# Top-64 attention: the threshold steering rounds counted from TensorE differences instead of ScalarE passes over the scores

## What is computed

```
scores = jnp.einsum('bhqd,bhkd->bhqk', Q, K) / jnp.sqrt(d)      # 32 x 16 x 256 x 256
topk_scores, topk_idx = jax.lax.top_k(scores, 64)
probs = jax.nn.softmax(topk_scores, axis=-1)
attn = einsum('bhqk,bhqkd->bhqd', probs, gather(V, topk_idx))
x = x + tanh(g_xattn) * (attn @ Wo.T + bo)        # attention of layernorm(x) and ctx
x = x + tanh(g_ffn) * ffn(layernorm(x))           # bf16 and fp8 rounding inside
```

## Time and profile before

| | |
|---|---|
| median of 3 runs | 3271.35 us (3269.1 to 3274.13) |
| the profiled execution | 3268.81 us, its span 3266.9 us |
| ScalarE busy | 2730.3 us, 84% |
| VectorE busy | 2691.6 us, 82% |
| TensorE busy | 1780.4 us, 54%, mean granted clock 0.717 |
| GpSimd busy | 966.1 us, 30% |

### The profile page before, as it was taken

One profiled execution on the slowest core, in us unless ns is written; L12 is line 12 of the kernel. 1 busy time (PEld: TensorE's weight loads), 2 busy tenths in 40 slices (PEclk: granted clock), 3 DMA queues, 4 the chain that ended last, 5 costly groups with the idle time before them and its releaser, 6 DMA issues.

```text
span 3266.9 us, 51511 instructions
## 1 busy us (share of the span) xinstructions
PE 1780.4 (54%) x7952; PEld 950.5 (29%) x7952; DVE 2691.6 (82%) x11883; ACT 2730.3 (84%) x9638; POOL 966.1 (30%) x1174
## 2 busy tenths in 40 slices
PE   3245555555465555455556556564556556454555
PEld 2122233332233233232323333332233223232222
DVE  1678888888888888888888888888888888888884
ACT  1888888998788898797889998988798788997983
POOL 5122223233222233232233223333223233232112
PEclk8567677777677777776667777767676767777777
DMA  4223332223333223331233333223333133331211
GB/s 70 38 43 60 49 47 52 52 49 63 52 52 54 45 49 63 52 55 34 48 64 56 60 48 56 48 48 64 53 49 55 33 62 61 55 54 33 40 24 46
DMA packets 451902, 166.43 MB, mean 51 GB/s; under 512 B 245616, under 2 KB 451440, under 8 KB 451520
## 3 DMA queue, kind: packets, MB, share of 16 engines
q1 hardware_dynamic: 451136, 162.38, 28.4%
q0 software_dynamic: 384, 0.33, 0.1%
HBM read 102.57 MB, written 59.24 MB: 50 GB/s over the span
## 4 chain that ended last, share of the span: by engine, by line
DVE 36%; ACT 30%; issue 17%; PE 14%; DVEq 2%; POOL 1%; ACTq 0%; DMA 0%; SPq 0%; POOLq 0%; another core or an unknown queue 0%
ACT act_junk L880 22%; DVE masked L1151 5%; DVE score_sb L1047 4%; PE ps_o L731 4%; DVE following L1157 4%; DVE masked L1146 3%; ACT unfit L891 3%; ACT pT_sb L900 2%; PE ps_a L684 2%; DVE X L1083 2%; PE ps_b L675 2%; PE ps_e L712 1%; PE ps_a L686 1%; DVE chord L1115 1%; PE ps_e L716 1%
## 5 line engine op out<-in xcount | busy, mean ns | idle before, releaser
L880 ACT ACTIVATE act_junk<-score_sb,X 128x256 int8<-128x256 f32 x3840 | 1892.1, 503 | 211.3 <-DVE X L1121 183.2
L712 PE MATMUL ps_e<-qs,ks 99*128 99x256 bf16 x1024 | 348.2, 350 | 1321.7 <-ACT pT_sb L900 1321.7
L731 PE MATMUL ps_o<-pT_sb,v_aug 128*32 128x256 f32 x2048 | 766.4, 514 | 0.5 <-ACT pT_sb L900 0.5
L880 ACT ACTIVATION_READ_ACCUMULATOR act_junk<-score_sb,X 128x1 f32 x3840 | 755.0, 197 | 0.0
L891 ACT ACTIVATE unfit<-score_sb,thr 128x256 bf16<-128x256 f32 x1024 | 463.1, 504 | 218.0 <-DVEq L1241 214.6
L1047 DVE TENSOR_SCALAR_CACHE_REDUCE score_sb<-ps_s 128x256 f32<-128x256 f32 x1024 | 418.8, 415 | 142.1 <-PE ps_s L698 140.0
L712 PEld LDWEIGHTS ps_e<-qs,ks 99*128 99x128 bf16 x1024 | 121.9, 119 | 1403.6 <-ACT unfit L891 1199.5
L1146 DVE TENSOR_SCALAR_CACHE_REDUCE masked<-score_sb,X 128x256 f32<-128x256 f32 x1024 | 426.3, 472 | 19.1 <-DVE x_res L1294 8.4
L1157 DVE MAX8 following<-masked 128x8 f32<-128x256 f32 x1024 | 357.7, 409 | 1.7 <-issue 0.7
L540 POOL CAST split<-proj 128x512 bf16<-128x512 f32 x64 | 48.0, 750 | 1042.8 <-ACT proj L866 1027.2
L716 PE MATMUL ps_e<-dropb,unfit 128*128 128x128 bf16 x2048 | 355.9, 273 | 0.0
(11 more groups left out here) (158 smaller groups left out, 3332.8 us busy)
## 6 DMA issues: line engine op xcount, KB each, us to landing
rows<-q_scr SPq DMA_DIRECT2D x192, 128.0 KB, 5.1
rows<-k_scr SPq DMA_DIRECT2D x192, 128.0 KB, 5.0
o_scr<-o_sb SPq DMA_DIRECT2D x128, 128.0 KB, 2.7
q_scr<-split SPq DMA_DIRECT2D x32, 384.0 KB, 2.7
k_scr<-split SPq DMA_DIRECT2D x32, 384.0 KB, 2.7
x_in<-in_x SPq DMA_DIRECT2D x32, 256.0 KB, 3.1
ctx_sb<-in_ctx SPq DMA_DIRECT2D x32, 256.0 KB, 2.7
v_scr<-proj SPq DMA_DIRECT2D x32, 256.0 KB, 5.8
```

Source lines behind the costliest of these rows:

```text
L712: nc.tensor.matmul(ps_e[:, n % 2, kc * TOK:(kc + 1) * TOK], ks[u][:, h, 8 * kc:8 * kc + 8, :].rearrange("d j t -> d (j t)"), qs[u][:, h, : ...
L731: ins = nc.tensor.matmul(ps_o[32 * c:32 * c + 32, half * TOK:(half + 1) * TOK], v_aug[p][:, 2 * h + kc, :], pT_sb[:, n % 2, kc * TOK:(kc + ...
L880: ins = nc.scalar.activation(act_junk[:, t, :], score_sb[:, slot, t, :], ACT.Sign, scale=-1.0, bias=X[slot % 2][:, 0, t:t + 1], accum_out= ...
```

## The change

ScalarE's counting passes over `score_sb` go. In a round TensorE transposes the thresholds (`transpose_thresholds`), ScalarE negates them into a 16x128 bf16 tile (`negate_thresholds`), and for each head TensorE forms the transposed scores in a bank of `ps_t` (`scores_by_key`) and adds the negated thresholds to all of them by a matmul whose stationary operand picks one row (`less_thresholds`). ScalarE takes one Sign of the 128x512 result into bf16 (`signs`), and TensorE sums the signs of every query over the keys with four matmuls against a column of ones (`tally`) into `ps_cnt`. VectorE reads the counts there. So that both sides see the same thresholds, they are kept as bf16 values (`stepped`, `started`).

The final counting moves from VectorE to ScalarE (`final_counts`, four tiles a round). VectorE's final tile is one product, (score <= threshold) x score, in place of the count and the 1024-wide subtraction, and two small steps are added to `final_thresholds`; a row whose 64th value is not positive counts as unsure.

PSUM is dealt out anew: three banks `ps_t` are shared by differences and exponents, counts and transposed thresholds share `ps_c`, and all projections, transposes and the second layer use the one bank `ps_a` in turn, which gives new waits between them. Exponents are two heads behind the masks in every engine. On TensorE a round is `count_round` with up to two exponents in it, then one piece of front or output work, two mixes, two scores and the transpose of the next thresholds. Projections of values run a batch earlier, and SP stores them earlier and moves `move_out` ahead of `move_values`. `settle` waits, in addition, for the final tiles of its round.

```diff
-MASK_LAG, MIX_LAG = 2, 4
+MIX_LAG = 2
+BANKS = 3
+SIGNS = 3
+JUNK = 4
...
+    return (GH * (GUIDES * (phase + 1) + r) + n) % SIGNS
...
+        ps_t = ps("ps_t", [P, BANKS, 512])
         ps_o = ps("ps_o", [P, 512])
         ps_a = ps("ps_a", [P, 512])
-        ps_b = ps("ps_b", [P, 512])
-        ps_x = ps("ps_x", [P, 512])
-        ps_xb = ps_x[:, 0:TOK].bitcast(BF16)
+        ps_c = ps("ps_c", [P, 512])
+        ps_xb = ps_a[:, 0:TOK].bitcast(BF16)
+        ps_xt = ps_c[0:GT, 0:P]
+        ps_cnt = [ps_c[:, P + GT * k:P + GT * (k + 1)] for k in range(2)]
+        ps_uns = ps_s[0:1, 0, 0:GT]
...
+                    store_values(b + 1)
                 if has(3):
                     load_front(b + 3)
                 move_maxima(b, u)
                 if has(2):
                     move_operands(b + 2)
...
+                if has(-1):
+                    move_out(b - 1)
                 if has(1):
                     move_values(b + 1, 1 - p)
-                if has(-1):
-                    move_out(b - 1)
...
+            def transpose_thresholds(i, slot, r):
+                pe.wait_ge(s_thr, GUIDES * i + r + 1)
+                pe.wait_ge(s_crd, GUIDES * i + r)
+                nc.tensor.transpose(ps_xt, X[slot][:, 0, :], ident[:]).then_inc(s_xt, 1)
+            def scores_by_key(u, g, n, bank):
+                h = head_of(g, n)
+                for kc in range(2):
+                    nc.tensor.matmul(ps_t[:, bank, kc * TOK:(kc + 1) * TOK],
+                                     ks[u][0:SPLITS, h, 8 * kc:8 * kc + 8, :].rearrange("d j t -> d (j t)"),
+                                     qs[u][0:SPLITS, h, :, :].rearrange("d j t -> d (j t)"), start=(kc == 0), stop=False,
+                                     skip_group_check=True)
+            def less_thresholds(i, r, n, bank):
+                if n == 0:
+                    pe.wait_ge(s_mx, GUIDES * i + r + 1)
+                both_chunks = minus_x[:].rearrange("t (o q) -> t o q", o=1).to_broadcast([GT, 2, P])
+                for jh in range(2):
+                    ins = nc.tensor.matmul(ps_t[:, bank, :].rearrange("p (c j q) -> p c j q", c=2, j=2)[:, :, jh, :],
+                                           identb[0:GT, 2 * n + jh:2 * n + jh + 1].to_broadcast([GT, P]), both_chunks,
+                                           start=False, stop=(jh == 1), skip_group_check=True)
+                ins.then_inc(s_R, 1)
+            def tally(i, par, r, n, buf):
+                pe.wait_ge(s_G, GUIDES * GH * i + GH * r + n + 1)
+                for jh in range(2):
+                    for kc in range(2):
+                        ins = nc.tensor.matmul(ps_cnt[par][:, 2 * n + jh:2 * n + jh + 1],
+                                               sign[:, buf, kc * TOK + jh * P:kc * TOK + jh * P + P], ones_b[:],
+                                               start=(kc == 0), stop=(kc == 1))
+                if n == GH - 1:
+                    ins.then_inc(s_cnt, 1)
...
+            def count_round(b, p, u, g, r, phase, first, second, last, middle):
+                i, slot = 2 * b + g, 2 * p + g
+                bank = [(phase + r + k) % BANKS for k in range(GH + 2)]
+                buf = [sign_buffer(phase, r, n) for n in range(GH)]
+                scores_by_key(u, g, 0, bank[0])
+                scores_by_key(u, g, 1, bank[1])
+                less_thresholds(i, r, 0, bank[0])
+                less_thresholds(i, r, 1, bank[1])
+                if last:
+                    exponent_taken(*last)
+                for n in (2, 3):
+                    scores_by_key(u, g, n, bank[n])
+                    less_thresholds(i, r, n, bank[n])
+                    tally(i, slot % 2, r, n - 2, buf[n - 2])
+                if first:
+                    exponents(*first, bank[4], False)
+                if middle:
+                    middle()
+                for n in (4, 5):
+                    tally(i, slot % 2, r, n - 2, buf[n - 2])
+                    scores_by_key(u, g, n, bank[n + 1])
+                    less_thresholds(i, r, n, bank[n + 1])
+                if first:
+                    exponent_taken(*first)
+                for n in (6, 7):
+                    scores_by_key(u, g, n, bank[n + 1])
+                    less_thresholds(i, r, n, bank[n + 1])
+                    tally(i, slot % 2, r, n - 2, buf[n - 2])
+                if second:
+                    exponents(*second, bank[9], False)
+                for n in (6, 7):
+                    tally(i, slot % 2, r, n, buf[n])
...
+                    for r in range(GUIDES):
+                        first, second = lagged(2 * r), lagged(2 * r + 1)
...
+                        middle = None
+                        if r == 0 and mixes:
+                            middle = lambda: sum_unsure(2 * mb + mg, 16 * (b + 1) + GH * g + 1 if has(1) else 16 * NB)
+                        if guided:
+                            count_round(cb, cp, cu, cg, r, phase, first, second, last, middle)
...
+                        if has(2) and (g, r) == (0, 0):
+                            transpose_tokens(b + 2)
+                        if has(2) and (g, r) == (0, 1):
+                            transpose_context(b + 2)
+                        if has(2) and (g, r) == (0, 2):
+                            project(b + 2, 0, 0)
+                        if has(-3) and (g, r) == (0, 3):
+                            ffn_transposes(b - 3, 2 * b + 5 if has(2) else 2 * NB, b + 2 if has(2) else NB, b - 2)
+                        if has(2) and (g, r) == (1, 0):
+                            project(b + 2, 1, b - 2)
+                        if has(-3) and (g, r) == (1, 1):
+                            ffn_matmul(b - 3, 2 * b + 6 if has(2) else 2 * NB)
+                        if has(-2) and (g, r) == (1, 2):
+                            out_project(b - 2, b - 2, 2 * b + 6 if has(2) else 2 * NB)
+                        if has(2) and (g, r) == (1, 3):
+                            project_values(b + 2, b - 1)
+                        if first:
+                            mix(*first)
+                        if second:
+                            mix(*second)
+                        for k in (2 * r + 2, 2 * r + 3):
+                            if k < GH and has(1):
+                                scores(b + 1, (u + 1) % OPS, g, k, 2 * b + g - 1 if k == 2 and mixes else None)
+                            if k >= GH and g == 0 and has(1):
+                                scores(b + 1, (u + 1) % OPS, 1, k - GH)
+                            if k >= GH and g == 1 and has(2):
+                                scores(b + 2, (u + 2) % OPS, 0, k - GH)
+                        if r < GUIDES - 1 and guided:
+                            transpose_thresholds(2 * cb + cg, 2 * cp + cg, r + 1)
+                        if r == GUIDES - 1 and has(1):
+                            transpose_thresholds(2 * (b + 1) + g, 2 * (1 - p) + g, 0)
...
-            def guide_counts(i, slot, r):
-                act.wait_ge(s_cnt, at(GUIDES * i + r))
-                act.wait_ge(s_thr, GUIDES * i + r + 1)
-                for t in range(ACT_TILES):
-                    ins = nc.scalar.activation(act_junk[:, t, :], score_sb[:, slot, t, :], ACT.Sign, scale=-1.0,
-                                               bias=X[slot % 2][:, 0, t:t + 1], accum_out=count[slot % 2][:, t:t + 1])
-                ins.then_inc(s_cnt, 1)
+            def negate_thresholds(i, r):
+                act.wait_ge(s_xt, GUIDES * i + r + 1)
+                nc.scalar.activation(minus_x[:], ps_xt, ACT.Copy, scale=-1.0).then_inc(s_mx, 1)
+            def signs(i, r, n, buf, bank):
+                act.wait_ge(s_R, GUIDES * GH * i + GH * r + n + 1)
+                nc.scalar.activation(sign[:, buf, :], ps_t[:, bank, :], ACT.Sign).then_inc(s_G, 1)
+            def final_counts(i, slot, t):
+                if t == 0:
+                    act.wait_ge(s_fin, FINAL * i + 1)
+                if t % JUNK == 0:
+                    act.wait_ge(s_fc, 4 * i + t // 4)
+                ins = nc.scalar.activation(act_junk[:, t % JUNK, :], score_sb[:, slot, t, :], ACT.Sign, scale=-1.0,
+                                           bias=X[slot][:, 0, t:t + 1], accum_out=final_count[:, t:t + 1])
+                if t % 4 == 3:
+                    ins.then_inc(s_fc, 1)
...
+            def round_of_signs(i, r, phase, i_final, final_slot, first, second, mixed):
+                bank = [(phase + r + k) % BANKS for k in range(GH + 2)]
+                if i is not None:
+                    negate_thresholds(i, r)
+                for n in range(GH):
+                    if i is not None:
+                        signs(i, r, n, sign_buffer(phase, r, n), bank[n if n < 4 else n + 1])
+                    if n == 3 and first:
+                        exps(*first, bank[4])
+                    if n == 3 and mixed:
+                        evacuate_mixed(*mixed)
+                    if n == 7 and second:
```

(71 more changed lines are left out.)

380 lines of the change are left out of this document (195 added, 185 removed).

## The result

| | before | after |
|---|---|---|
| median | 3270.22 us (3266.8 to 3274.13, 4 runs) | 3739.13 us (3727.18 to 3747.62, 4 runs) |
| profiled execution, span | 3266.9 us | 3733.4 us |
| TensorE busy, mean granted clock | 54%, 0.717 | 94%, 0.665 |
| ScalarE busy | 84% | 67% |
| VectorE busy | 82% | 59% |

The ratio is 1.1431, 95% interval 1.1395 to 1.1467: 14% slower. The prediction was 3145 us, range 2970 to 3340. It is wrong in sign and size.

The account below looks back on a forecast made before the run. Bound by the loop of ScalarE's counts and VectorE's threshold update, 12.05 us a round; after, 31.5 batches of 90.15 us (2840), repairs 71, ahead 170, behind 61, plus 1.9: forecast 3145 us, range 2970 to 3340.

Parts of the forecast that it names:

- The clock: TensorE after the change: longest pause about 1 us, so priced at clock 1.00, 256 bf16 columns in 0.11 us.
- the clock doesn't hold: Rival: TensorE at clock 0.50, 18 us a round, 4800 us; a third of rounds so, above 3600; chance 0.03.
- The pitch of matmuls: TensorE, per head: scores by key 0.22 us and thresholds on 16 rows 0.22 us, two matmuls of 256 columns each.
- The tallies: TensorE, per head: four weight loads with one-column matmuls, 0.06 us a pair, 0.24 us together.
- my lower bound of 0.03: TensorE's tallies: least cost of 0.03 us a pair, nothing but issue, half of the quickest pair.
- The first rival: Tallies make TensorE the bound, slower than before: 3520 us at 0.107 us a pair; with partial forms, chance 0.26.
- The load of 107 ns: TensorE's tallies: the skill page's weight load for 128 columns, 107 ns at any clock; the forecast followed a trace row instead.
- the sum: Whole kernel: 31.5 batches of 90.15 us, repairs 71, ahead 170, behind 61: span 3142 us, 11.27 a round without repairs.
- A repair: Slow selection of unsure tiles: each holds a round for about 10 us, 7 x 10.2 = 71 us.
- The wait for the masks: ScalarE waiting for VectorE's masks once a head group: 3.4 us a group goes, except in a repair.
- GpSimd's thin cover: Key operands on GpSimd: about 3 us of cover; were it gone, 1 to 3 us a batch, up to 95 us.
- VectorE off the path: VectorE's round gets about 1.8 us lighter, but that work isn't on the path while it waits for counts.

Follow-up runs that it names:

- e11_no_repairs: Repairs of unsure tiles left out, against the changed kernel with its threshold matmuls padded to 128 rows: 3101.66 us.
- e8_final_on_vector: Final counting put back on VectorE, against the changed kernel with its threshold matmuls padded to 128 rows: 3265.45 us.

## Why the prediction was wrong

**The clock: the step that failed.** "After, the longest pause is the wait for an update, about 1 us, so I price at 1.00." The premise held, TensorE has almost no pause outside the repairs, and the clock was 0.665. The rows that I rested on the earlier trace rows show a burst of exponents, scores, mixes and a projection, of 96 to 128 rows; I carried their clock over to matmuls of 16 rows and one column. The rival "the clock doesn't hold" had the right mechanism, with a price above 3600 us for a third of the rounds; I gave it 0.03 because work without pause had raised the clock in the earlier trace rows, and here work without pause didn't. The Trainium skill, page "TensorE: Matmul & The Clock Gate", section "What's actually happening", ties the clock to how busy the engine has been. If the busy share of the profile is taken for that, this case doesn't agree: TensorE is recorded as busy for 94% of the span at 0.665, and with 128 rows for 80% at 0.918.

**The pitch of matmuls: a term mis-sized.** 0.22 us for two of 256 columns was taken from a stream of like operands. With 16 or 64 rows next to 96 it is 0.32; 16 groups a round, 1.6 us of TensorE. The step from 64 to 96 rows, in which it goes, is worth 141 us with its share of clock; what it cost at 16 rows wasn't measured. The Trainium skill, the same page, Part 3, section "The mechanism", has weight loads overlap matmuls in flight only where the row groups differ, or where the load goes to the background weight buffer. Here loads are hidden between 96 and 128 rows, which share row groups, and not between 96 and 16 or 64, which share them too, so the row groups alone don't say it, and why it is so stays open.

**The tallies: mis-sized the other way.** 0.06 a pair was taken, 0.024 to 0.028 measured, just under my lower bound of 0.03. The first rival (slower because of the tallies, 0.26) ended on the right side for a wrong reason. The load of 107 ns that the prediction quotes from the Trainium skill, page "TensorE: Matmul & The Clock Gate", section "LDWEIGHTS (loading the stationary operand)", is near what one record shows (105 ns on average for the tallies' loads), but it is not what one costs in a row: four loads and matmuls start and are done with in 0.11 us.

**What stood.** With a clock of 0.921, hidden loads and no repairs, e11_no_repairs allows the sum to be tested: its masks are released from 193.7 to 3023.5 us, 11.23 us a round; forecast 11.27. Some of that agreement is luck: the tallies gave back 1.0 us of TensorE a round, and the clock wasn't 1.00. A repair was priced at 10.2 us and costs 9.6; 7 were forecast, 5 or 8 are seen. The wait for the masks went as said. GpSimd's thin cover held: scores waited for keys once, at the start. VectorE's busy time fell by 1.97 us a round (1.8 told), though a masked product takes 0.42 us and not 0.35; ScalarE's fell by 0.84 (1.2 told), and by 1.15 with 128 rows.

**VectorE off the path: only in part.** e8_final_on_vector gives VectorE back 272.7 us of work, 1.1 us a round (the rest of the 1.8 is the tile that it counted itself), and costs 87 us, 0.35 us a round, although ScalarE gets 438.6 us lighter.

**The whole gap.** Span forecast 3142, measured 3733.4: 591 us. Ahead of the first release 215.9 instead of 170 (46), behind the last 75.6 instead of 61 (14), and 252 rounds of 13.66 instead of 11.55 with repairs (531). Widening the operand alone takes 561 us of time back.

What stays open: the clock was varied by rows and by added work, not by columns or waits one at a time, so what else holds it was not found. Nor was it tried whether another order, with the wide f32 work between the narrow matmuls, would do without the padding.

## What to carry to other kernels

A TensorE that shows busy in every slice can run at half its clock for most of the time: read the granted clock of the stretch that would be bound, and price matmuls that use few rows at the lower level unless a like row says otherwise. Where an operand has few rows, padding it with zero rows to the full height costs no time by itself and gave here a higher clock and hidden weight loads, 561 us together. Before work is moved to an engine because it has idle time, find out at what speed it will run the new kind of work.

## What the runs showed of the hardware

- Mean granted clock against rows of the threshold operand: 0.665 (16), 0.809 (64), 0.842 (96), 0.915 (128), though the added rows hold only zeros.
- TensorE recorded as busy for 94% of the span had a mean clock of 0.665; at 80% busy, with 128 rows, it had 0.918.
- 4096 useless matmuls of 128 rows and 128 columns made the kernel 133 us faster (clock 0.665 to 0.816).
- Two 256-column bf16 matmuls of 96 rows, start to start: 0.32 us at full clock where the matmuls beside them have 16 or 64 rows, 0.22 where they have 96 or 128.
- A 128x128 bf16 weight load with a one-column matmul costs 0.024 to 0.028 us in a row of them.
